# VectorE takes a norm ahead of a sum, the queries' norms move one row block ahead, and the first transfers change their order

## The chip, the cores and the metric

One core of one Trainium2 chip. The metric is device time in microseconds for one execution of the whole program. Engines: PE (TensorE), ACT (ScalarE), DVE (VectorE), POOL (GpSimd), SP (SyncE, which only issues transfers here). They run their own instruction streams and meet at semaphores.

## The reference

One layer of cross-attention and one of experts, all in float32. Cut to the part that the change touches:

```
x: 16 batches x 56 queries x 256;  context: 16 x 1500 x 256, the first 257 rows "image", the other 1243 "text"
q = rms_norm(layernorm(x) @ q_w + q_b) * nq_s          # 16 heads of 128; the mean is over all 2048 columns
for part in (image, text):
    k = rms_norm(part @ k_w + k_b) * nk_s              # 16 heads of 128
    v = part @ v_w + v_b
    out += softmax(q k^T / sqrt(128)) v                # softmax over the rows of that part alone
x = x + out @ o_w + o_b
x = x + experts(layernorm(x))                          # top 4 of 32 experts, and a shared one
```

## The kernel before

The keys and values are never formed. For each head the queries are multiplied by the key weights ("absorbed queries", `u`), so that scores are `context @ u`, and averages are taken over the raw context rows; the value weights follow later. A key row's norm comes from a product of the context row with a Gram matrix of the weights. Float32 operands are split into a high and a low part (fp32r), and each product is three matmuls: high by high, high by low, low by high.

**Stages.** `prologue` (layer norm, Gram matrices), `project` (queries, `u`), the batch loop in `attend`, `outputs`, `experts`. The loop runs from 255 to 1460 us of the span.

**Projection.** `project` goes through 16 heads. For each head, `absorb` computes `u` in four row blocks (two halves of 448 columns each), over four PSUM banks in turn; `order` fixes which unit takes which bank, and `claim` waits until the unit four places before has been copied out. ACT copies half 0 and DVE half 1 (`copy_u`). Near the end three small pieces stand between row blocks: `flip` transposes the sums of squares of the queries, from which DVE and POOL make the norms; `wide` spreads the norms over all partitions, copied out by ACT to `q_rms_wide`; `flat` finds the largest bound on a score, from which DVE judges (`is_safe`) whether the loop must run with maxima. From `q_rms_wide` DVE also makes `beta`, the part of the scores that comes from the key bias. SP stores `beta` in DRAM, loads it back spread over the partitions (`beta_wide`, one transfer for image, one for text), and then copies head 15's first batch of `u` to `u_raw` (L518). POOL scales and splits `u_raw` (`first_rows`) and lets PE begin.

**The loop.** A batch has 13 context tiles of 128 rows: tiles 0 to 2 image (tile 2, `LONE`, has one row), 3 to 12 text. Each tile has two units (448 of the 896 columns of heads by queries), so a batch has 26 steps. At step s the engines do, each in its own order, written out by hand:

- PE: scores of unit s (6 matmuls); at some steps a sum over partitions (`sums`, L1190 and L1191, 2 matmuls); at even steps the Gram product of tile s/2+1 (5 matmuls); the average of unit s-2 (6 matmuls).
- ACT: the exponential of unit s-1, once rounded (`p_high`), once in place; at even steps the high part of a tile (`c_high`).
- DVE: `take` of unit s-1: `p_low` (L1370), the running `p_sum` (L1426 or L1423), and the `seed` that puts beta in a PSUM bank for the scores three units on (L1381); at even steps the `norm` of tile s/2+1 (L1395), which reads the Gram product from PSUM and `c_twice` from SBUF; at steps 1, 2 (text of the batch before) and 7, 8 (image) `split_sum`: the cast `p_sum_high` (L1434), then `p_sum_low` (L1370, two SBUF inputs).
- POOL: at even steps `key_root` (L1558), the power -1/2 of the norm's result, then at most steps one long piece over 896 columns (scaling or splitting `u`, or scaling averages: L1583, L1608, L1621); at odd steps `c_low` (L1564) and `c_twice` (L1577) of a tile.

The Gram product and the sums share one PSUM bank. The sum at step 3 or 9 therefore waits until the norm of step 2 or 8 has read the bank (`norm_summed`), and the sums at 5 and 11 for the norms of 4 and 10. These are `TEXT_SUMS = (3, 5)` and `IMAGE_SUMS = (9, 11)`. DVE takes the norm after `take`, except at step 6, where it comes first.

Of the kernel before, what the change touches and what calls it, by code (L numbers as in the profile page):

```python
# [413 lines left out]
def project(nc, qw_in, kw_in, psum, ident, minus_half, zeros, small, key_scale, bias_high, bias_low, x_high, x_low,  # L414
# [4 lines left out]
    with ctx:  # L419
# [29 lines left out]
        for h in range(H):  # L449
            if h + 2 < H:  # L450
                order += [("q", h + 2, half) for half in range(2)]
            if h == H - 1:
                order += [("wide", half) for half in range(2)]
            for r in range(4):
                if h == H - 2 and r == 2:
                    order += [("flip",)]
                if h == H - 1 and r == 1:
                    order += [("flat",)]
                order += [("u", h, r, half) for half in range(2)]
# [23 lines left out]
        def sync(sp):  # L483
            def load_q(h):
                if h >= LOADS:
                    sp.wait_ge(wq_split, h - LOADS + 1)
                sp.dma_start(wq_stage[:, h % LOADS, :], qw_in[h, :, :]).then_inc(wq_loaded[h % LOADS], 16)

            def load_k(h):
                if h >= LOADS:  # L490
                    sp.wait_ge(wk_split, h - LOADS + 1)
                sp.dma_start(wk_stage[:, h % LOADS, :], kw_in[h, :, :]).then_inc(wk_loaded[h % LOADS], 16)

            def store_u(h):
                sp.dma_start(u_dram[h, :, :, :], u_stage[:, h % U_RING, :, :])\
                    .then_inc(u_stored[h % U_RING], 16)

            for h in range(LOADS):
                load_q(h)
                if h < 2:  # L500
                    load_k(h)
            for h in range(2, LOADS):
                load_k(h)
            for h in range(H):
                if h + LOADS < H:
                    load_q(h + LOADS)
                if 0 < h and h + LOADS - 1 < H:
                    load_k(h + LOADS - 1)
                if h == H - 4:
                    first_tiles[0](sp)  # L510
                if h == H - 1:
                    sp.wait_ge(beta_ready, 1)
                    sp.dma_start(beta_dram, beta[:, :]).then_inc(beta_stored, 16)
                    sp.wait_ge(beta_stored, 16)
                    first_tiles[6](sp)
                sp.wait_ge(u_act, 4 * (h + 1))
                sp.wait_ge(u_dve, 4 * (h + 1))
                sp.dma_start(u_raw[:, :, h * S:(h + 1) * S], u_stage[:, h % U_RING, :, 0:S])\  # L518
                    .then_inc(first_stored[h % U_RING], 16)
                if h < H - U_RING:  # L520
                    store_u(h)

        def sync_stores(sp, s, heads=range(H - U_RING, H)):
# [5 lines left out]
        def tensor(pe):  # L529
# [58 lines left out]

            absorb(H - 2, range(2))
            at = claim(("flip",))  # L590
# [6 lines left out]
            first_tiles[1](pe)  # L597
            absorb(H - 2, range(2, 4))
            for half in range(2):
# [7 lines left out]
                last.then_inc(wide_done, 1)  # L607
            pe.wait_ge(wk_split, H)
            absorb(H - 1, range(1))
            at = claim(("flat",))  # L610
            pe.wait_ge(bound_step, 4)
            nc.tensor.matmul(psum[0:1, at, 0:TOK], bound_max[:, :], ident[0:TOK, 0:TOK], start=True, stop=True)\
                .then_inc(bound_flat, 1)
            absorb(H - 1, range(1, 4))
            pe.wait_ge(beta_ready, 1)
# [4 lines left out]
        def scalar(act):  # L620
# [47 lines left out]
            for h in range(H):  # L668
                if h + 2 < H:
                    take(h + 2)  # L670
                if h + 1 < H:
                    weights_k(h + 1)
                if h + 3 < H:
                    weights_q(h + 3)
                if h == H - 1:
                    for half in range(2):
                        act.wait_ge(wide_done, half + 1)
                        nc.scalar.activation(q_rms_wide[:, cols(half)], psum[:, bank["wide", half], 0:HALF], ACT.Copy)\
                            .then_inc(wide_copied, 1)
                copy_u(h, range(4))  # L680
                if h == H - 3:
                    first_tiles[2](act)

        def vector(dve):
# [39 lines left out]
            for h in range(H):  # L724
# [8 lines left out]
                if h < H - 2:  # L733
# [4 lines left out]
                          psum[0:ROWS_SQ, SUMS:SUMS + 2, 0:HALF]).then_inc(sums_copied, 1)  # L738
            copy_u(H - 2, range(2))
            dve.wait_ge(flipped, 1)  # L740
# [3 lines left out]
                .then_inc(bound_step, 1)  # L744
            copy_u(H - 2, range(2, 4))
            first_tiles[4](dve)
            for step in (1, 2):
# [4 lines left out]
            V.tensor_reduce(bound_max[:, :], bound_sq[:, :], mybir.AxisListType.X, ALU.max).then_inc(bound_step, 1)  # L752
            copy_u(H - 1, range(1))
            dve.wait_ge(bound_flat, 1)
# [8 lines left out]
                            q_rms_wide[0:2 * H, :].rearrange("p (h n) -> p h n", h=2), ALU.mult).then_inc(beta_ready, 1)  # L763
            copy_u(H - 1, range(1, 4))

# [8 lines left out]
def attend(nc, ctx_in, qw_in, kw_in, psum, ident, minus_half, zeros, small, key_scale, bias_high, bias_low, x_high,  # L774
# [4 lines left out]
    with ctx:  # L779
# [29 lines left out]

        def first_betas(sp):  # L810
            for s in range(2):
                sp.dma_start(beta_wide[:, s, :].rearrange("p (h q) -> p h q", h=H),
                             beta_rows[s, :, 0:S].partition_broadcast(P)).then_inc(beta_loaded[s], 16)

# [124 lines left out]
        def _(sp):  # L939
# [159 lines left out]
            with sp.If(unsafe(sp)):  # L1099
                sp.wait_ge(first_split, 9)  # L1100
                for s in range(2):
                    project_stores(sp, s)
                    stored(s)
                with sp.Fori(0, B) as it:
                    maxima(it)
                sp.wait_ge(max_listed, 32 * B + CREDIT["max_listed"])
                for s in range(2):
                    load_u(0, s, u_loaded[s])
                    sp.dma_start(beta_wide[:, s, :].rearrange("p (h q) -> p h q", h=H),
                                 beta_rows[s, :, 0:S].partition_broadcast(P)).then_inc(beta_again, 16)  # L1110
                batches(sp, body_of(False), tail)
            with sp.Else():
# [5 lines left out]
        def _(pe):  # L1118
# [136 lines left out]
            with pe.If(unsafe(pe)):  # L1255
                with pe.Fori(0, B) as it:
                    maxima(it)
                pe.wait_ge(rank_zeroed, 2)
                batches(pe, body_of(False), tail)
            with pe.Else():  # L1260
# [100 lines left out]
        def _(dve):  # L1361
# [99 lines left out]
            def body(it, has_prev, has_next):  # L1461
                for step in range(UNITS):
                    if has_prev and step == 0:
                        take(it - 1, UNITS - 1, True)

                    norms_first = step == 2 * LONE + 2
                    if norms_first:
# [84 lines left out]
        def _(gp):  # L1552
# [114 lines left out]
            for i in range(3):  # L1667
                for k, x in enumerate(first_stored):
                    gp.wait_ge(x, 16 * len([h for h in range(heads[i + 1]) if h % U_RING == k]))
                first_rows(slice(heads[i], heads[i + 1]), 3 * i)  # L1670
            gp.wait_ge(first_split, 9)
            with gp.If(unsafe(gp)):
                with gp.Fori(0, B) as it:
# [3 lines left out]
                gp.wait_ge(first_split, 12)  # L1677
            gp.sem_inc(u_scaled, 2)
            gp.sem_inc(u_high_ready, 2)
            gp.sem_inc(u_split, 2)  # L1680
            batches(gp, body, tail)
# [560 lines left out]
```

## Time and profile before

| | us |
|---|---|
| median of 3 runs | 1937.68 (1935.91 to 1941.32) |
| profiled execution | 1937.42 |
| its span | 1935.3 |
| PE busy | 1774.7 (92%) |
| DVE busy | 1328.5 (69%) |
| POOL busy | 1099.4 (57%) |
| ACT busy | 977.4 (51%) |

The span is the time from the first to the last instruction. Busy time is the sum of an engine's instructions; what counts for the end is which wait ends last at each place, which the timelines below show for one batch of the loop.

### The profile page before, as it was taken

Reading aid. Unit: us, or ns where it says so; the run is one execution under the profiler, and the core shown is the slowest. Engines: PE = TensorE matmul, PEld = TensorE weight load, DVE = VectorE, ACT = ScalarE, POOL = GpSimd, SP = SyncE. Lnnn points to the kernel's source line nnn. Section 1 sums busy time; section 2 is a strip of 40 time slices with the busy share of each in tenths; the row PEclk is TensorE's granted clock in tenths of the full one; section 3 lists DMA queues with packets and bytes.
Section 4 is the critical chain, followed back from the end, with each engine's and each line's share of the span. In section 5 each row is a group of like instructions: output and inputs, shape, how many; then the busy total and the mean of one; then the engine's idle time right before and its main releaser. Section 6 shows DMA issues by size and latency. Waiting matters only on the chain. (4 is left out here: it accounts for less than half of the span.)

```text
span 1935.3 us, 30607 instructions
## 1 busy us (share of the span) xinstructions
PE 1774.7 (92%) x8863; PEld 1563.6 (81%) x8863; DVE 1328.5 (69%) x2522; ACT 977.4 (51%) x1627; POOL 1099.4 (57%) x955
## 2 busy tenths in 40 slices
PE   7899969999999999999999999999992998699998
PEld 7566769889888898898898898898882887588887
DVE  4444457877877777777777768777772565577776
ACT  3444435555655655655555555556552563244443
POOL 1000267778778787788788787787862331133332
PEclk9999989999999999999999999999996999699999
DMA  3355555455555565554464564555435782133332
GB/s 109 126 201 198 193 166 117 109 115 123 117 118 119 125 122 116 121 129 121 101 147 101 113 132 120 114 119 124 101 84 189 250 274 86 61 118 108 121 108 78
DMA packets 417215, 251.17 MB, mean 130 GB/s; under 512 B 350123, under 2 KB 368683, under 8 KB 415372
## 3 DMA queue, kind: packets, MB, share of 16 engines
q1 hardware_dynamic: 417164, 250.54, 50.7%
q8 instruction: 26, 0.43, 0.1%
q14 instruction: 25, 0.20, 0.0%
HBM read 187.70 MB, written 60.10 MB: 128 GB/s over the span
## 5 line engine op out<-in xcount | busy, mean ns | idle before, releaser
L1297 ACT ACTIVATE p_high<-psum,key_rms 128x448 fp32r<-128x448 f32 x384 | 245.1, 638 | 393.1 <-PE psum L1128 393.1
L1370 DVE TENSOR_TENSOR p_low<-psum,p_high 128x448 fp32r<-128x448 f32 x384 | 237.7, 619 | 184.4 <-ACT psum L1299 178.9
L1126 PE MATMUL psum<-u_high,c_high 128*128 128x448 f32 x832 | 307.2, 369 | 26.1 <-DVE psum L1381 13.8
L1128 PE MATMUL psum<-u_high,c_low 128*128 128x448 f32 x832 | 305.6, 367 | 0.0
L1127 PE MATMUL psum<-u_low,c_high 128*128 128x448 f32 x832 | 305.2, 367 | 0.0
L1126 PE MATMUL psum<-p_high,c_high 128*128 128x448 f32 (+1 forms) x768 | 283.5, 369 | 4.1 <-DVE p_low L1370 4.1
L1127 PE MATMUL psum<-p_low,c_high 128*128 128x448 f32 (+1 forms) x768 | 282.2, 367 | 0.0
L1128 PE MATMUL psum<-p_high,c_low 128*128 128x448 f32 (+1 forms) x768 | 281.9, 367 | 0.0
L1564 POOL TENSOR_TENSOR c_low<-stage,c_high 128x512 fp32r<-128x512 f32 x208 | 276.7, 1330 | 0.0
L1381 DVE COPY psum<-beta_wide 128x448 f32<-128x448 f32 x416 | 260.9, 627 | 21.7 <-DMA beta_wide<-absorbed_biases 5.8
L1558 POOL TENSOR_TENSOR key_rms<-key_ms,minus_half 128x1 f32<-128x1 f32 x209 | 117.5, 562 | 244.2 <-DVE key_ms L1395 241.8
L1299 ACT ACTIVATE psum<-psum,key_rms 128x448 f32<-128x448 f32 x384 | 232.6, 606 | 0.0
L1951 POOL TENSOR_TENSOR scaled_gate<-gated,p_wide 128x448 f32<-128x448 f32 x66 | 86.6, 1311 | 193.1 <-ACT gated L2046 157.5
L1426 DVE TENSOR_TENSOR p_sum<-psum,p_sum 128x448 f32<-128x448 f32 (+1 forms) x320 | 196.2, 613 | 0.0
L1126 PEld LDWEIGHTS psum<-u_high,c_high 128*128 128x128 f32 x832 | 156.9, 189 | 46.6 <-DVE psum L1381 16.6
L1127 PEld LDWEIGHTS psum<-u_low,c_high 128*128 128x128 f32 x832 | 157.1, 189 | 13.3
L1128 PEld LDWEIGHTS psum<-u_high,c_low 128*128 128x128 f32 x832 | 157.0, 189 | 13.3
L1577 POOL TENSOR_TENSOR c_twice<-stage,c_low 128x256 f32<-128x256 f32 x208 | 157.9, 759 | 16.4 <-POOL c_low L1564 2.4
L1126 PEld LDWEIGHTS psum<-p_high,c_high 128*128 128x128 f32 (+1 forms) x768 | 143.9, 187 | 17.5 <-DVE p_low L1370 7.5
L1128 PEld LDWEIGHTS psum<-p_high,c_low 128*128 128x128 f32 (+1 forms) x768 | 144.0, 187 | 12.9
L1127 PEld LDWEIGHTS psum<-p_low,c_high 128*128 128x128 f32 (+1 forms) x768 | 144.8, 189 | 10.0
L1395 DVE CUSTOM_DVE_ANT_0 junk<-psum,c_twice 128x257 bf16<-128x257 f32 x208 | 89.0, 428 | 92.9 <-POOL c_twice L1577 74.4
(240 smaller groups left out, 3844.4 us busy)
## 6 DMA issues: line engine op xcount, KB each, us to landing
stage<-in_ctx SPq DMA_DIRECT2D x210, 256.0 KB, 2.8
averages<-o_raw SPq DMA_DIRECT2D x64, 448.0 KB, 5.2
o_stage<-averages SPq DMA_DIRECT2D x32, 896.0 KB, 5.6
u_raw<-absorbed_queries SPq DMA_DIRECT2D x60, 448.0 KB, 5.5
absorbed_queries<-u_stage SPq DMA_DIRECT2D x14, 1792.0 KB, 6.8
beta_wide<-absorbed_biases SPq DMA_DIRECT2D x32, 448.0 KB, 5.1
recip_wide<-reciprocals SPq DMA_DIRECT2D x32, 448.0 KB, 4.1
p_wide<-probs_by_expert SPq DMA_DIRECT2D x32, 448.0 KB, 3.6
```

What stands on the lines that cost most here:

```text
L1126: nc.tensor.matmul(out, high, rhigh, start=start, stop=False, **kw)
L1127: nc.tensor.matmul(out, high, rlow, start=False, stop=False, **kw)
L1128: return nc.tensor.matmul(out, low, rhigh, start=False, stop=stop, **kw)
L1297: nc.scalar.activation(p_high[:, probs_slot(u), :], src, ACT.Exp, scale=key_rms[:, t:t + 1])
L1299: nc.scalar.activation(out, src, ACT.Exp, scale=key_rms[:, t:t + 1]).then_inc(exp_done, 1)
L1370: return nc.vector.tensor_tensor(out, a, b, ALU.subtract)
L1381: nc.vector.tensor_copy(psum[:, bank_of(u), 0:HALF], beta_wide[:, s, cols_of(half)])\
L1395: nc.vector.tensor_tensor_reduce(out=junk[:, :], in0=psum[:, GRAM, 0:DIM + 1], in1=c_twice[:, slot(t, TWICE_RING), :], scale=1.0 / INNER, ...
L1426: added = nc.vector.tensor_tensor(total, part, total, ALU.add)
L1558: nc.gpsimd.tensor_tensor(key_rms[:, t:t + 1], key_ms[:, t:t + 1], minus_half[:, 0:1], ALU.pow)\
L1564: nc.gpsimd.tensor_tensor(c_low[:, k, :], stage[:, st, :], c_high[:, k, :].bitcast(F32), ALU.subtract)\
L1577: nc.gpsimd.tensor_tensor(c_twice[:, slot(t, TWICE_RING), 0:DIM], stage[:, st, nat], c_low[:, k, nat].bitcast(F32), ALU.add).then_inc(stag ...
```

## The change

In `attend`, `norms_first` now holds at steps 2, 4, 8 and 10 beside 6. In `project`, `flip`, `wide` and `flat` each stand one row block earlier on PE, with their partners on ACT and DVE. `first_betas` is called once for each half: the image half where both stood, the text half after the last `u_raw`. POOL's three increments move ahead of its branch; where the branch is taken (it isn't with this data), SP and PE now wait for the last split.

```
             for r in range(4):
-                if h == H - 2 and r == 2:
+                if h == H - 2 and r == 1:
                     order += [("flip",)]
-                if h == H - 1 and r == 1:
+                if h == H - 2 and r == 3:
+                    order += [("wide", half) for half in range(2)]
+                if h == H - 1 and r == 0:
                     order += [("flat",)]
...
                     sp.wait_ge(beta_stored, 16)
-                    first_tiles[6](sp)
+                    first_tiles[6](sp, 0)
                 sp.wait_ge(u_act, 4 * (h + 1))
                 sp.wait_ge(u_dve, 4 * (h + 1))
                 sp.dma_start(u_raw[:, :, h * S:(h + 1) * S], u_stage[:, h % U_RING, :, 0:S])\
...
+            first_tiles[6](sp, 1)
...
-            absorb(H - 2, range(2))
+            absorb(H - 2, range(1))
             at = claim(("flip",))
...
-            absorb(H - 2, range(2, 4))
+            absorb(H - 2, range(1, 3))
             for half in range(2):
                 at = claim(("wide", half))
...
-            pe.wait_ge(wk_split, H)
-            absorb(H - 1, range(1))
+            absorb(H - 2, range(3, 4))
             at = claim(("flat",))
             pe.wait_ge(bound_step, 4)
...
-            absorb(H - 1, range(1, 4))
+            pe.wait_ge(wk_split, H)
+            absorb(H - 1, range(4))
...
-                    norms_first = step == 2 * LONE + 2
+                    norms_first = step % 2 == 0 and (step + 1 in TEXT_SUMS + IMAGE_SUMS or step == 2 * LONE + 2)
                     if norms_first:
                         norm(*ahead(it, step // 2 + 1))
...
             gp.wait_ge(first_split, 9)
+            gp.sem_inc(u_scaled, 2)
+            gp.sem_inc(u_high_ready, 2)
+            gp.sem_inc(u_split, 2)
             with gp.If(unsafe(gp)):
...
-            gp.sem_inc(u_scaled, 2)
-            gp.sem_inc(u_high_ready, 2)
-            gp.sem_inc(u_split, 2)
             batches(gp, body, tail)
```

On DVE, `copy_u` of head 14 is cut at 1 and 3 instead of 2, and that of head 15 is one piece at the end; on ACT the two copies of `wide` stand before block 3 of head 14.

## Rows read from the trace of the kernel before

**Rows 1.** Busy table, loop: us, busy PE, PEld, DVE, ACT, POOL, clock, DMA.
```profile
360.00:1480.00 1120.00, 1053.05 (x5473) 959.80 (x5471) 834.70 (x1697) 623.41 (x1067) 866.48 (x760) 0.99 0.54 117
```
**Rows 2.** Who waited for whom on PE in the loop: us, times, longest.
```profile
PE psum L1190 <- DVE key_ms L1395: 34.0, 31, 1.6
```
**Rows 3.** Timeline, casts beside POOL: start, duration, engine, line; brackets: idle before it.
```profile
486.21 0.74 POOL L1577 TENSOR_TENSOR c_twice<-stage,c_low 128x256 f32<-128x256 f32 x1
486.40 0.81 DVE L1434 CAST p_sum_high<-p_sum 128x448 fp32r<-128x448 f32 x1
...
489.84 0.39 DVE L1434 CAST p_sum_high<-p_sum 128x448 fp32r<-128x448 f32 x1
...
490.00 0.63 POOL L1558 TENSOR_TENSOR key_rms<-key_ms,minus_half 128x1 f32<-128x1 f32 x1 [3.05 <-DVE key_ms L1395]
...
490.26 0.62 DVE L1370 TENSOR_TENSOR p_sum_low<-p_sum,p_sum_high 128x448 fp32r<-128x448 f32 x1
...
490.61 2.27 POOL L1608 TENSOR_TENSOR u_low<-u_raw,u_high 128x896 fp32r<-128x896 f32 x1
```
**Rows 4.** Timeline of steps 2 to 4 around the text sum.
```profile
487.78 0.62 DVE L1370 TENSOR_TENSOR p_low<-psum,p_high 128x448 fp32r<-128x448 f32 x1
...
489.50 0.42 DVE L1395 CUSTOM_DVE_ANT_0 junk<-psum,c_twice 128x257 bf16<-128x257 f32 x1
...
489.98 0.47 PE L1190 MATMUL psum<-p_sum_high,ones_r 128*128 128x448 f32 x1 [0.67 <-DVE key_ms L1395]
...
493.54 0.37 PE L1126 MATMUL psum<-p_high,c_high 128*128 128x448 f32 x1
...
494.98 0.43 DVE L1395 CUSTOM_DVE_ANT_0 junk<-psum,c_twice 128x257 bf16<-128x257 f32 x1 [0.55 <-POOL c_twice L1577]
```
**Rows 5.** Timeline of steps 5 to 8.
```profile
497.05 1.57 DVE L1426 TENSOR_TENSOR p_sum<-lone_probs,p_sum 1x448 f32<-1x448 f32 x1
...
498.09 1.69 POOL L1564 TENSOR_TENSOR c_low<-stage,c_high 128x512 fp32r<-128x512 f32 x1
...
500.62 0.43 DVE L1395 CUSTOM_DVE_ANT_0 junk<-psum,c_twice 128x257 bf16<-128x257 f32 x1 [2.01 <-POOL c_twice L1577]
...
501.65 0.47 PE L1126 MATMUL psum<-u_high,c_high 128*128 128x448 f32 x1 [0.81 <-DVE psum L1381]
```
**Rows 6.** Timeline of steps 8 to 10 around the image sum.
```profile
506.02 0.62 DVE L1370 TENSOR_TENSOR p_low<-psum,p_high 128x448 fp32r<-128x448 f32 x1
...
507.74 0.42 DVE L1395 CUSTOM_DVE_ANT_0 junk<-psum,c_twice 128x257 bf16<-128x257 f32 x1
...
508.22 0.48 PE L1190 MATMUL psum<-p_sum_high,ones_r 128*128 128x448 f32 x1 [1.48 <-DVE key_ms L1395]
...
508.85 2.29 POOL L1583 TENSOR_TENSOR u_raw<-u_raw,rms_batch 128x896 f32<-128x896 f32 x1
...
511.79 0.37 PE L1126 MATMUL psum<-p_high,c_high 128*128 128x448 f32 x1
```
**Rows 7.** Timeline, end of the projection.
```profile
227.79 1.07 DVE L737 COPY square_sums<-psum 33x896 f32<-33x896 f32 x1
```
**Rows 8.** Timeline of the hand-over, and the transfers of L518.
```profile
242.04 2.27 SPq L812 DMA_DIRECT2D beta_wide<-absorbed_biases  x2
242.17 0.62 DVE L716 COPY u_stage<-psum 128x448 f32<-128x448 f32 x1 [0.59 <-PE psum L534]
...
244.41 3.09 SPq L518 DMA_DIRECT2D u_raw<-u_stage  x1
...
251.64 0.42 POOL L1583 TENSOR_TENSOR u_raw<-u_raw,q_rms_wide 128x112 f32<-128x112 f32 x1 [5.11 <-DMA u_raw<-u_stage]
...
252.48 0.42 POOL L1603 TENSOR_TENSOR u_low<-u_raw,u_high 128x112 fp32r<-128x112 f32 x1
...
255.06 0.74 PE L1126 MATMUL psum<-u_high,c_high 128*128 128x448 f32 x1 [12.31 <-POOLq L1680]
...
DMA to landing us min/median/max: 2.2/2.3/7.1
```

More of the change, by code:

```diff
@@ L451, in project @@
                 order += [("q", h + 2, half) for half in range(2)]
-            if h == H - 1:
-                order += [("wide", half) for half in range(2)]
             for r in range(4):
-                if h == H - 2 and r == 2:
+                if h == H - 2 and r == 1:
                     order += [("flip",)]
-                if h == H - 1 and r == 1:
+                if h == H - 2 and r == 3:
+                    order += [("wide", half) for half in range(2)]
+                if h == H - 1 and r == 0:
                     order += [("flat",)]
@@ L674, in scalar @@
                     weights_q(h + 3)
-                if h == H - 1:
+                copy_u(h, range(4) if h != H - 2 else range(3))
+                if h == H - 2:
                     for half in range(2):
@@ L679, in scalar @@
                             .then_inc(wide_copied, 1)
-                copy_u(h, range(4))
+                    copy_u(h, range(3, 4))
                 if h == H - 3:
@@ L738, in vector @@
                           psum[0:ROWS_SQ, SUMS:SUMS + 2, 0:HALF]).then_inc(sums_copied, 1)
-            copy_u(H - 2, range(2))
+            copy_u(H - 2, range(1))
             dve.wait_ge(flipped, 1)
@@ L744, in vector @@
                 .then_inc(bound_step, 1)
-            copy_u(H - 2, range(2, 4))
+            copy_u(H - 2, range(1, 3))
             first_tiles[4](dve)
@@ L752, in vector @@
             V.tensor_reduce(bound_max[:, :], bound_sq[:, :], mybir.AxisListType.X, ALU.max).then_inc(bound_step, 1)
-            copy_u(H - 1, range(1))
+            copy_u(H - 2, range(3, 4))
             dve.wait_ge(bound_flat, 1)
@@ L763, in vector @@
                             q_rms_wide[0:2 * H, :].rearrange("p (h n) -> p h n", h=2), ALU.mult).then_inc(beta_ready, 1)
-            copy_u(H - 1, range(1, 4))
+            copy_u(H - 1, range(4))
         def gpsimd(gp):
@@ L808, in first_loads, with first_betas @@
                 sp.dma_start(stage[:, t, :], ctx_in[t, :, :]).then_inc(ctx_loaded[t], 16)
[L810 to L813, printed above, removed]
+        def first_betas(sp, s):
+            sp.dma_start(beta_wide[:, s, :].rearrange("p (h q) -> p h q", h=H),
+                         beta_rows[s, :, 0:S].partition_broadcast(P)).then_inc(beta_loaded[s], 16)
         def first_gram(pe):
@@ L1110, in _ @@
                                  beta_rows[s, :, 0:S].partition_broadcast(P)).then_inc(beta_again, 16)
+                sp.wait_ge(first_split, 12)
                 batches(sp, body_of(False), tail)
@@ L1258, in _ @@
                 pe.wait_ge(rank_zeroed, 2)
+                pe.wait_ge(first_split, 12)
                 batches(pe, body_of(False), tail)
```

## The prediction

> **What bounds the kernel now.** I read the busy table by stage first, then who waits for whom in the batch loop, then one batch in order of time, then the hand-over into the loop. In the middle of the loop PE is busy 1053.05 of 1120 us, far more than any other engine [rows 1]: it sets the pace, and only what makes PE idle is worth anything. The list of waits names the largest item: 34.0 us in 31 waits, in which the sum's first matmul (L1190) waits for the norm (L1395) [rows 2]. It falls on the first of each pair of sums: 0.67 us at step 3 (text, 15 times) and 1.48 us at step 9 (image, 16 times) [rows 4, 6]. The same places come back in every batch, so one batch stands for all. A wait costs a little more than its idle time: the first matmul after it is recorded 0.10 longer (0.47 for 0.37), and the idle time is counted from the end of the record before, where a matmul otherwise starts every 0.2 us [rows 4]. That is 0.10 + 0.17 each. The ceiling of the loop part is therefore 34 us plus 31 times 0.27, some 42 us.
>
> **Norm first at steps 2, 4, 8 and 10.** No instruction is added; DVE does the same norm at another place, and there it takes the same 0.34 us (489.50 to the next start at 489.84 [rows 3, 4]).
> At step 8 DVE would start it where p_low of unit 7 starts now, at 506.02, and end it at 506.5; PE is ready for the sum at 508.22 - 1.48 = 506.74 [rows 6]. So the 1.48 goes; the norm's two inputs are there by then in the timeline. At step 2 it starts at 487.78 instead of 489.50, with its c_twice done at 486.95 [rows 3], and the 0.67 goes as well [rows 4]. If nothing else moved, this would be the whole 42 us.
> But something else moves. key_root on POOL follows the norm by 0.5 us, and POOL's next long instruction follows key_root by 0.61 (490.00 to 490.61 [rows 3]). At step 2 that is u_low, at step 8 the scaling of u_raw; each takes 2.0 us from where it really starts (u_low is recorded at 490.61 but ends 2.00 after the vector instruction beside it, 490.88) [rows 3, 6]. Today both follow the cast p_sum_high, because the norm stands right before that cast. With the norm first, u_low would run from about 488.8 to 490.9, while DVE still reaches the cast at 489.84. DVE and POOL block each other here. The trace shows it three times: a cast of 0.39 takes 0.81 when it starts at 486.40 inside c_twice (486.21 to 486.95), ending 0.26 after it [rows 3]; the p_sum of the lone row, started at 497.05, ends at 498.62, and c_low, started at 498.09, takes 1.69 and ends 1.16 after that [rows 5]; and key_root, started inside the cast at 490.00, ends at 490.63, in the middle of p_sum_low [rows 3]: POOL had its turn between the two vector instructions.
> This is what the Trainium skill says in "SBUF — State Buffer", section "Who interferes with whom": VectorE in a two-port mode or with two SBUF inputs, and GpSimd, exclude each other for a whole instruction, and the one that issued first goes first. By that rule the trace agrees, and it speaks against this change. Whose turn comes next after a pair, the page doesn't say.
> So at step 2: the cast is held from 489.84 to 490.9 and ends at 491.2. POOL's next instruction, c_low, is by then waiting and takes its turn, 1.16 us, to 492.35. p_sum_low (L1370) then ends at 492.85, not at 490.88, and p_low of unit 2, next on DVE, starts at 492.8 and ends at 493.4. average(2) begins on PE at 493.54 today [rows 4]; without the sum's stall it could begin at 492.6, and now it begins at 493.45. The stall is only handed on.
> Step 8 is the same: the scaling of u_raw runs from 507.05 to 509.2 over the cast at 508.08, c_low takes its turn to 510.6, p_sum_low ends at 511.1, p_low of unit 8 at 511.65; average(8) begins at 511.7, where it begins at 511.79 today [rows 6]. Nothing won.
> What stays: DVE comes to norm 4 (step 4, now first) at 494.5, not at 494.98 [rows 4], for c_twice has come earlier too. key_root, u_low and c_low follow on POOL, so c_twice for step 6 and its norm (500.62, after 2.01 us of waiting for it) come 0.5 to 0.7 earlier, and with them the seed for which PE waits 0.81 at 501.65 [rows 5]. I take 0.6 us in each of 15 batches: 9 us. Step 10 moves likewise and costs nothing: p_low of unit 9 comes after its norm, and average(9) stands over 2 us later in PE's order.
> Bounds: above nothing, if POOL's turn is longer than I think (rival below); at most 42 us plus up to 0.8 us of the wait at 501.65 in 16 batches, 55 us. I stay near the low end because the rows of blocking are the nearest ones.
>
> **Norms of the queries one row block ahead.** The transposition of the square sums (flip), the widened norms (wide) and the flat maximum each move ahead by one row block; PE has the same matmuls before banks_set. The flip may wait for the copy of the square sums, 1.07 us from 227.79 [rows 7]; only its last few tenths are uncovered by the six matmuls of block 0. I cost it at 0, between -1 and +1. What it gives is beta ready about one block earlier: six matmuls at 0.2 us each, 1.2 us, of which I take 1.1. Behind the moved pieces wait ACT's and DVE's copies of block 3 of head 14, and behind those SP's u_raw of head 14 (1 to 2 us later); POOL needs it only after two long pieces of work on heads 0 to 7, so this is hidden.
>
> **First transfers.** Today both beta_wide transfers (issued from 242.04) are ahead of the last u_raw (L518), which SP issues at 244.41 over 3.09 us, and which lands after 7.1 us; other u_raw transfers land in 2.2 to 2.3 [rows 8]. DVE's last copy ends at 242.79, so SP could issue it at 242.85. Then only one beta is ahead of it. Two betas cost 7.1 - 2.3 = 4.8, one 2.4: landing at 242.85 + 2.3 + 2.4 = 247.6 instead of 251.64, 4.1 us. Beta 0 itself, issued 1.1 earlier and alone, must be there and copied twice, which gives about the same time. Bounds: 1 us (only beta's earlier store counts) and 5 us. The text beta comes last, needed first at the seed of unit 6, ten and more us later: free.
> The three sem_inc of POOL move ahead of its branch: u_low ends at 252.90 and PE starts at 255.06 [rows 8]; these 2.16 us go. PE then starts 2 us ahead of POOL's first instruction of the loop, which is the first to be wanted at step 2, so I keep all of it. Sum 6.2, of which I take 5.5: the tile loads on SP move only 1 to 2 us, and the fourth may be late for ACT. The first matmul of the loop takes 0.74 us, twice 0.37, so TensorE stands at the lower of its two levels, 1.2 GHz, after 12.31 us of idle time [rows 8]; some 6 or 7 us of idle time remain, and I leave that price as it is.
> The waits for first_split 12 are in the branch that isn't taken: 0.
>
> **Sum.** The profiled execution took 1937.42 us for a span of 1935.3; the median of the runs is 1937.68, the same within 0.3. 1937.4 - 9 - 5.5 = 1922.9, so 1923 us.
>
> **Rivals.**
> A, the vector pair goes as one: after the blocked cast DVE also gets p_sum_low before POOL's c_low. p_low of unit 2 then ends at 492.4, in time, p_low of unit 8 at 510.65, 1.1 ahead of today. Per batch 1.3 (text, with norm 6) + 1.0 = 2.3, 35 us in all: 1937.4 - 35 - 5.5 = 1897. For it: DVE's two instructions stand 0.42 apart; against it: key_root at 490.00, which got in between [rows 3]. 0.14.
> B, no collision (POOL's instruction comes later than I think, or doesn't block a cast): near the 55 us bound, less 2: 1937.4 - 53 - 5.5 = 1879. Against it the 0.81 us cast [rows 3]. 0.10.
> C, the start alone: norm 6 comes no earlier, because c_low or c_twice is held by DVE instructions that now stand beside it: 1937.4 - 5.5 = 1932. 0.14.
> D, slower: p_sum_low waits for c_low and for c_twice behind it (0.74 [rows 3]). It decides once POOL issues c_twice before the port goes back. Then average(2) begins 0.6 and average(8) 0.7 later than today, and norm 6 0.2 later; PE keeps 0.9 of it per batch: 1937.4 + 14 - 5.5 = 1946. For it: my margin at both averages is only 0.1 us. Against it: c_low needs its own result's semaphore before c_twice. 0.10.
>
> **Chances and range.** Forecast 0.52, A 0.14, B 0.10, C 0.14, D 0.10. The range 1894 to 1934 holds the forecast, A and C, 0.80. The forecast's own range, with the start between 2 and 7 us and the loop between 5 and 14, is 1917 to 1931. Changes under 0.3% (5.8 us, below 1931.9) can't be told from none here. Faster: forecast, A, B and half of C, 0.83; same: the other half of C, 0.07; slower: D, 0.10.
>
> **What would show it.** After the change the row "L1190 waits for key_ms" must be gone or near it. By the forecast PE idles instead before average(2) and average(8), put down to p_low (L1370), some 0.8 and 1.5 us in each batch, p_sum_high (L1434) takes over 1 us at steps 2 and 8 instead of 0.39, and p_sum_low about as long again. The period of a batch, from one image sum to the next, falls by 0.6 us; by A it falls by 2.3, by B by over 3, by C not at all, and by D it rises. The first matmul of the loop (255.06) should come at 249 to 250. The forecast is wrong if p_sum_high keeps its 0.39 at both places, or if a new wait stands before the scores instead of the averages.

## The result, and the profile after

The changed kernel takes 1921.17 us (median of 4 runs, 1920.35 to 1922.58), the kernel before 1939.5 in the same comparison (4 runs, 1935.91 to 1942.01). The ratio is 0.9908, with a 95% interval of 0.9888 to 0.9927. The forecast was 1923 in a range of 1894 to 1934. The profiled span went from 1935.3 to 1919.1 us, so 16.2 us went; the stretches add up as follows, each read from the start of a PE instruction in the two timelines.

| Stretch | before, us | after, us | difference |
|---|---|---|---|
| start to first matmul of the loop | 255.06 | 249.72 | -5.3 |
| first matmul of the loop to last image sum | 1203.92 | 1192.31 | -11.6 |
| last image sum to the end | 476.32 | 477.07 | +0.8 |

The third row lies between 473 and 479 in the profiles of all kernels below, whatever was changed, so it isn't a cost of the change. The loop's part is -0.71 in the period of a batch, 75.04 to 74.33 (from one image sum to the next, the mean of the first 14; the batch shown below has 433.19 to 508.22 [rows 6] and 425.40 to 499.71), times 15, which is -10.6 us, and -1.0 in batch 0 (28.05 to 27.02 from the first matmul to the first image sum).

First the page of after, in the total busy time of each engine:

```profile
span 1919.1 us, 30607 instructions
...
PE 1777.4 (93%) x8863; PEld 1562.5 (81%) x8863; DVE 1373.3 (72%) x2522; ACT 970.6 (51%) x1627; POOL 1101.5 (57%) x955
```

Every count is as before. Yet DVE is busy 44.8 us longer (1328.5 before) on the same 2522 instructions: something holds it inside its instructions. The next row is the middle of the loop, with the columns of [rows 1]:

```profile
360.00:1480.00 1120.00, 1055.76 (x5467) 959.68 (x5466) 876.32 (x1692) 620.61 (x1068) 867.78 (x759) 0.99 0.55 121
```

DVE rose from 834.70 to 876.32, POOL hardly from 866.48 to 867.78. Which instructions took DVE's time, the groups of DVE by line show (count, then busy time and mean ns, then idle time before them):

```profile
L1373 DVE TENSOR_TENSOR p_sum_low<-p_sum,p_sum_high 128x448 fp32r<-128x448 f32 x64 | 69.6, 1088 | 2.2
...
L1437 DVE CAST p_sum_high<-p_sum 128x448 fp32r<-128x448 f32 x64 | 59.4, 928 | 0.0
```

The cast had a mean of 483 ns and p_sum_low of 626. Half of the 64 of each are the second halves of a sum, and these are the ones that grew. The two groups grew by 58.1 us; other DVE instructions became shorter, among them the `p_sum` of the lone row, 1.57 us [rows 5] before and 1.01 now.

Then who waits for whom on PE in the loop (us in total, times, longest us). Beside the row of [rows 2], the kernel before had these two:

```profile
PE psum L1126 <- DVE psum L1381: 13.8, 16, 1.4
PE psum L1126 <- DVE p_low L1370: 4.1, 16, 0.3
```

After the change:

```profile
PE psum L1128 <- DVE p_low L1373: 32.9, 47, 1.3
...
PE psum L1128 <- DVE psum L1384: 4.7, 17, 1.1
```

The row of [rows 2], 34.0 us in 31 waits for the norm, is gone without remainder. In its place stand 32.9 us in 47 waits of the averages for `p_low`, which were 4.1 us before; and the 13.8 us in 16 waits for the seed (the copy of beta into a PSUM bank) came down to 4.7. Together, -34.0 + 28.8 - 9.1 is 14.3 us less of recorded idle time, beside the 11.6 us by which the loop is shorter. One batch shows how. This is the text sum of the batch, on three engines, and answers to [rows 3 to 5]:

```profile
481.59 0.42 DVE L1398 CUSTOM_DVE_ANT_0 junk<-psum,c_twice 128x257 bf16<-128x257 f32 x1
482.10 0.55 POOL L1561 TENSOR_TENSOR key_rms<-key_ms,minus_half 128x1 f32<-128x1 f32 x1 [1.34 <-DVE key_ms L1398]
482.61 2.13 POOL L1611 TENSOR_TENSOR u_low<-u_raw,u_high 128x896 fp32r<-128x896 f32 x1
482.95 0.37 PE L1192 MATMUL psum<-p_sum_high,ones_r 128*128 128x448 f32 x1
483.65 1.34 DVE L1437 CAST p_sum_high<-p_sum 128x448 fp32r<-128x448 f32 x1
484.70 1.44 POOL L1567 TENSOR_TENSOR c_low<-stage,c_high 128x512 fp32r<-128x512 f32 x1
485.03 1.60 DVE L1373 TENSOR_TENSOR p_sum_low<-p_sum,p_sum_high 128x448 fp32r<-128x448 f32 x1
487.21 0.47 PE L1128 MATMUL psum<-p_high,c_high 128*128 128x448 f32 x1 [0.66 <-DVE p_low L1373]
488.26 0.42 DVE L1398 CUSTOM_DVE_ANT_0 junk<-psum,c_twice 128x257 bf16<-128x257 f32 x1
493.77 0.43 DVE L1398 CUSTOM_DVE_ANT_0 junk<-psum,c_twice 128x257 bf16<-128x257 f32 x1 [0.64 <-POOL c_twice L1580]
494.80 0.48 PE L1128 MATMUL psum<-u_high,c_high 128*128 128x448 f32 x1 [0.19 <-DVE psum L1384]
```

Read it from the top. The norm is early and the sum on PE (482.95) no longer waits. But POOL's `u_low` now starts 1.04 us before the cast, and the cast needs 1.34 instead of 0.39: it ends at 484.99, 0.25 after `u_low` (484.74). Now `c_low` goes first and ends at 486.14, 1.15 after the cast; `p_sum_low`, though recorded from 485.03, ends at 486.63. So `p_low` behind it is late and PE waits 0.66 before average(2). What is won comes later: the norm of step 6 waits 0.64 for `c_twice`, where it waited 2.01 [rows 5], and PE waits 0.19 for the seed of the scores, where it waited 0.81.

The image sum, steps 8 and 9, answers to [rows 6]:

```profile
499.71 0.41 PE L1192 MATMUL psum<-p_sum_high,ones_r 128*128 128x448 f32 x1
500.20 2.14 POOL L1586 TENSOR_TENSOR u_raw<-u_raw,rms_batch 128x896 f32<-128x896 f32 x1
501.24 1.34 DVE L1437 CAST p_sum_high<-p_sum 128x448 fp32r<-128x448 f32 x1
502.27 1.46 POOL L1567 TENSOR_TENSOR c_low<-stage,c_high 128x512 fp32r<-128x512 f32 x1
502.62 1.60 DVE L1373 TENSOR_TENSOR p_sum_low<-p_sum,p_sum_high 128x448 fp32r<-128x448 f32 x1
504.81 0.47 PE L1128 MATMUL psum<-p_high,c_high 128*128 128x448 f32 x1 [1.28 <-DVE p_low L1373]
```

The 1.48 before the sum has become 1.28 before average(8), by the same three steps.

The hand-over into the loop answers to [rows 8]:

```profile
243.44 0.61 SPq L518 DMA_DIRECT2D u_raw<-u_stage  x1
244.09 0.63 SPq L813 DMA_DIRECT2D beta_wide<-absorbed_biases  x1
248.16 1.68 DVE L1384 COPY psum<-beta_wide 128x448 f32<-128x448 f32 x3 [4.80 <-DMA beta_wide<-absorbed_biases]
248.19 0.42 POOL L1586 TENSOR_TENSOR u_raw<-u_raw,q_rms_wide 128x112 f32<-128x112 f32 x1 [2.27 <-DMA u_raw<-u_stage]
249.03 0.42 POOL L1606 TENSOR_TENSOR u_low<-u_raw,u_high 128x112 fp32r<-128x112 f32 x1
249.72 0.74 PE L1128 MATMUL psum<-u_high,c_high 128*128 128x448 f32 x1 [6.41 <-POOLq L1677]
```

POOL waits 2.27 us for the last `u_raw` instead of 5.11, and PE begins 0.27 after POOL's `u_low` ends (249.45), where 2.16 us lay between them. PE's idle time fell from 12.31 to 6.41. The price of the low clock behind it stayed nearly the same: the granted clock is 0.50, TensorE's lower level of 1.2 GHz, up to a matmul 5.7 us behind the first in the kernel before (260.78) and 5.0 behind it here (254.69), and the 40th matmul after the first starts 10.17 and 10.26 us after it.

### The profile page after: what moved, and what is told of

Same layout as the page of the kernel before. It is cut to its first block and busy times, and to the rows that moved or that the text cites. A ratio compares the mean times of both kernels' runs of the same rounds, so it can differ in the third digit from the quotient of the medians.

```text
span 1919.1 us, 30607 instructions
## 1 busy us (share of the span) xinstructions
PE 1777.4 (93%) x8863; PEld 1562.5 (81%) x8863; DVE 1373.3 (72%) x2522; ACT 970.6 (51%) x1627; POOL 1101.5 (57%) x955
## 5 line engine op out<-in xcount | busy, mean ns | idle before, releaser
L1128 PE MATMUL psum<-p_high,c_high 128*128 128x448 f32 (+1 forms) x768 | 288.6, 376 | 32.9 <-DVE p_low L1373 32.9
L1580 POOL TENSOR_TENSOR c_twice<-stage,c_low 128x256 f32<-128x256 f32 x208 | 169.5, 815 | 16.3 <-POOL c_low L1567 2.4
L1624 POOL TENSOR_TENSOR o_raw<-o_raw,recip_wide 128x896 f32<-128x896 f32 x64 | 136.0, 2126 | 13.9 <-DMA recip_wide<-reciprocals 13.9
```

What stands on the lines that cost most here:

```text
L1128: nc.tensor.matmul(out, high, rhigh, start=start, stop=False, **kw)
L1580: nc.gpsimd.tensor_tensor(c_twice[:, slot(t, TWICE_RING), 0:DIM], stage[:, st, nat], c_low[:, k, nat].bitcast(F32), ALU.add).then_inc(stag ...
L1624: nc.gpsimd.tensor_tensor(at, at, recip_wide[:, s, cols].unsqueeze(1).to_broadcast([P, 2, HALF]), ALU.mult).then_inc(o_scaled, 1)
```

## The experiments

Unless said otherwise a kernel is timed beside the kernel before, on the same chip, and the ratio is to that one. "Period" is the time from one image sum to the next, as the mean of the first 14.

**The two parts apart.** The first kernel is the kernel before with the order of the norms alone; the second is the changed kernel with that line put back.

```
-                    norms_first = step == 2 * LONE + 2
+                    norms_first = step % 2 == 0 and (step + 1 in TEXT_SUMS + IMAGE_SUMS or step == 2 * LONE + 2)
```

> The kernel before with only the norms ahead of the sums (steps 2, 4, 8, 10). My account: the port between VectorE and GpSimd hands the stall on, the batch period falls by 0.69 us as in the changed kernel, so the loop gives 11 us and the total is 0.9943 of before (1926 to 1930). The first matmul of the loop stays at 255. Rival, that the loop gains only because the start moved: under 3 us, ratio above 0.998.

> The changed kernel with the norms back behind take (only step 6 first): what is left is the projection's order, the transfers and the three increments. My account: first loop matmul at 249.7 instead of 255.1, batch period 75.05 as before, total 5.3 us less, ratio 0.9972. Rival, that the later tile loads give the start back: first matmul at 249.7, but total within 2 us of before.

Norms alone: 1923.37 us, ratio 0.9929 (0.9902 to 0.9956), period 74.32, first matmul of the loop at 255.00 after 12.15 us. Start alone: 1930.7, ratio 0.9964 (0.9954 to 0.9974), period 75.02, first matmul at 251.01 after 6.32. Both totals are lower than expected; in the two profiles the stretch after the last image sum is 473.1 and 473.8 us for 476.3 before, and neither edit touches it. The first matmul of start alone is later than the 249.7 expected because the projection ended later in its profile, at 243.92 for 242.54 (start of its last record). Both parts are worth something by themselves, and the shares 0.71% and 0.36% come to 1.07% against 0.92% for both together, which the intervals allow. Rival C (the start alone matters) falls. Inside batch 0, from the first matmul to the first image sum, the changed kernel takes 27.02 us and norms alone 26.16. That isn't a price of the earlier start as such: start alone takes 27.89, not more than the 28.05 before. The changed kernel has one wait for a seed more there, 0.41 us at 269.31; what brings it is open.

**Does POOL's place matter?** In the changed kernel POOL waits, at step 2 before `split_u` and at step 8 before `scale_u`, until the pair of DVE is through. The norm stays first; only the collision goes.

```
+                    if step == 2:
+                        gp.wait_ge(sum_split, 4 * it + CREDIT["sum_split"])
...
+                    if has_next and step == 8:
+                        gp.wait_ge(sum_split, 4 * it + 2 + CREDIT["sum_split"])
```

> The changed kernel, with GpSimd's long piece at step 2 and at step 8 made to wait for p_sum_low of the second half, so that it can't run over the cast. Port alone (rival): casts back at 0.39 us, average(2) and average(8) in time, 2 us less per batch, some 32 us under the changed kernel. My account has a second bound, GpSimd's own chain norm - key_root - long piece - c_low - c_twice - next norm, 5.3 us long: started later by these waits, it makes norm 4 and norm 10 wait 2 to 2.6 us on VectorE, and the period is 74.5 to 75.0, so 2 to 10 us above the changed kernel though nothing is blocked at the casts.

1934.17 us, ratio 0.9979 (0.9966 to 0.9991), period 75.23. The cast is back at its old length, at this place in the timeline (and 483 ns in the mean):

```profile
484.57 0.39 DVE L1437 CAST p_sum_high<-p_sum 128x448 fp32r<-128x448 f32 x1
...
490.00 0.43 DVE L1398 CUSTOM_DVE_ANT_0 junk<-psum,c_twice 128x257 bf16<-128x257 f32 x1 [2.66 <-POOL c_twice L1580]
490.49 0.47 PE L1192 MATMUL psum<-p_sum_high,ones_r 128*128 128x448 f32 x1 [0.56 <-DVE key_ms L1398]
```

So the long cast is `u_low`'s and the scaling's doing, shown by taking them away. But the loop gained nothing from its shorter DVE instructions: POOL is late, the norm of step 4 waits 2.66 us for `c_twice`, and PE waits again for norms, now before the second sums at 5 and 11. The waits of this kernel, PE's and DVE's own:

```profile
PE psum L1192 <- DVE key_ms L1398: 25.8, 30, 1.3
...
DVE junk L1398 <- POOL c_twice L1580: 124.3, 104, 2.7
```

DVE's waits for `c_twice` are 11.6 us in the changed kernel and 74.4 before. The gain of the edit thus is POOL's earlier chain, not the norm's place; with POOL's chain held back it is gone. The period came out 0.2 above that of before and beyond what was expected (74.5 to 75.0). POOL is held back a little more here than it was before the change: its `u_low` starts 1.90 us after the sum's first matmul (485.77 to 483.87), where it really started 0.90 after it (490.88 to 489.98 [rows 3, 4]), and that matmul had been stalled by 0.67. Whether this is the whole 0.2 isn't shown.

**Which half of the edit?** Norm first at 2, 4 and 6 only.

```
+                    norms_first = step % 2 == 0 and (step + 1 in TEXT_SUMS or step == 2 * LONE + 2)
```

> The changed kernel without the image half of the edit (norm first at 2, 4 and 6, behind take at 8 and 10). My account: at step 8 the stall was only handed from the sum to average(8), so the 1.48 us wait of L1190 comes back, the 1.28 us wait before average(8) goes, and the total is within 2 us of the changed kernel. Rival, that the image norms are worth their wait: 16 times 1.5, 20 us or more above it.

1923.6 us, ratio 0.9923 (0.9899 to 0.9947), period 74.36, against 74.33 with both. PE's waits:

```profile
PE psum L1192 <- DVE key_ms L1398: 23.9, 16, 1.6
...
PE psum L1128 <- DVE p_low L1373: 13.9, 32, 0.7
```

One name of a wait, 23.9 us in 16, is exchanged for the other (19.0 us in 15: 13.9 and 32 times here, 32.9 and 47 in the changed kernel), and no time goes with it; of the 2.4 us in the total 1.8 stand ahead of the loop (first matmul at 251.51 for 249.72). As long as the collision is there, the image half of the edit is worth nothing.

**Take the collision away by moving DVE's pair, not POOL.** Here the second halves' split stands right behind the norm, ahead of `take`. POOL waits for that norm (`key_root` first), so its long instruction can't start before the pair does.

```
                     if norms_first:
                         norm(*ahead(it, step // 2 + 1))
+                    if has_prev and step == TEXT_SUM_SPLIT[1]:
+                        split_sum(it - 1, TEXT, 1)
+                    if step == IMAGE_SUM_SPLIT[1]:
+                        split_sum(it, IMAGE, 1)
                     if step >= 1:
                         take(it, step - 1, has_next)
```

(The old places keep the first halves only.)

> The changed kernel with one more move: at steps 2 and 8 VectorE splits the second half's sum (p_sum_high, p_sum_low) right behind the norm and ahead of take, so that the pair runs in the 1.0 us before GpSimd's long piece starts. My account (the port hands the stall on): both casts back at 0.39 us, p_sum_low at 0.62, average(2) and average(8) without a wait, norm 4 and norm 6 about 1 us earlier; new small waits before average(1) and average(7), whose p_low now comes 0.95 us later. Period 72.7 (72.3 to 73.3), some 26 us under the changed kernel, about 1895. Rival, that p_low is late because of what DVE has in front of it and not because of the port: the wait moves to average(1) and average(7) whole and the period stays at 74.3.

1900.07 us, ratio 0.9804 (0.9787 to 0.982), period 73.01, inside the expected 72.3 to 73.3. In its timeline the pair goes through undisturbed and `u_low` starts behind the cast:

```profile
478.21 0.42 DVE L1398 CUSTOM_DVE_ANT_0 junk<-psum,c_twice 128x257 bf16<-128x257 f32 x1
478.56 0.39 DVE L1437 CAST p_sum_high<-p_sum 128x448 fp32r<-128x448 f32 x1
478.98 0.63 DVE L1373 TENSOR_TENSOR p_sum_low<-p_sum,p_sum_high 128x448 fp32r<-128x448 f32 x1
479.33 2.27 POOL L1615 TENSOR_TENSOR u_low<-u_raw,u_high 128x896 fp32r<-128x896 f32 x1
...
497.05 0.47 PE L1128 MATMUL psum<-p_high,c_high 128*128 128x448 f32 x1 [0.83 <-DVE p_low L1373]
```

The cast's mean is 482 ns and that of `p_sum_low` 626. The move brings 1.32 us per batch (74.33 less 73.01), nearly twice what the edit had brought. The collision cost more than that, since the move has a price of its own: PE's waits for `p_low` fell only to 17.5 us in 33, and 0.83 of them stands at the image's place in each batch, because the pair is now ahead of `take`.

The next kernel is the same with the norm first at steps 2, 6 and 8, no longer at 4 and 10.

```
+                    norms_first = step in (2, 6, 8)
```

> As e5_split_ahead, but at steps 4 and 10 the norm stands behind take again. Asks whether these two are worth anything. My account: VectorE reaches norm 4 about 1 us after its c_twice is there, GpSimd's chain to norm 6 starts 1 us later, and PE's wait for the seed of unit 8 is 0.7 to 1 us longer: period 73.4 to 73.8, 12 to 16 us above e5_split_ahead. Rival, that only steps 2 and 8 count: the same as e5_split_ahead within 2 us.

1913.29 us, ratio 0.9864 (0.9847 to 0.988), period 73.74. The order at 4 and 10 is worth 0.74 us per batch, and PE shows where:

```profile
PE psum L1128 <- DVE p_low L1373: 17.5, 33, 0.8
...
PE psum L1128 <- DVE psum L1384: 12.1, 16, 1.1
```

The waits for `p_low` are the same; the seed of unit 6 is late, 12.1 us in 16, as it was before the change (0.72 at 492.21 in the batch shown, where the norm of step 6 waits 2.00 for `c_twice` at 491.18). So the path of the gain is norm of step 4, POOL's chain, `c_twice`, norm of step 6, seed. Steps 4 and 10 weren't taken apart; the wait that comes back is the one behind step 4.

**POOL's turn between the pair.** The second halves' low part is left out, in the changed kernel: `p_sum_low` and its matmul (0.4 us of matmuls per batch). The output lacks the low part of those sums. If `c_low` took its turn only because the pair came in two instructions, the long cast stays and the rest goes.

```
                 nc.vector.tensor_copy(p_sum_high[:, half, :], ...).then_inc(sum_high_ready, 1)
...
+                if half == 1:
+                    dve.sem_inc(sum_split, 1)
+                    return
```

> The changed kernel without p_sum_low of the second halves and without the matmul that reads it (the sums of the second halves lose their low part). Takes away the instruction that waits for c_low's turn; the blocked cast stays at 1.34 us. My account: average(2) and average(8) start without a wait, 0.93 and 1.55 us, 0.4 us of matmuls less, the seed's wait gone: period 71.2 (71.0 to 71.8). If the cast's own blocking were what makes p_low late, the waits would shrink only by p_sum_low's plain 0.55 us: period 73.0 or more.

1878.67 us, ratio 0.9695 (0.9679 to 0.9712), period 71.47. The cast, here at step 2, is as long as in the changed kernel, and PE waits for `p_low` no more than before the change:

```profile
476.21 1.33 DVE L1441 CAST p_sum_high<-p_sum 128x448 fp32r<-128x448 f32 x1
...
PE psum L1128 <- DVE p_low L1377: 4.4, 17, 0.3
```

(The first line is the timeline's, the second the list of waits.) Without its second member the pair costs PE nothing: the 0.95 us of the cast alone are hidden. Of the 2.86 us by which the period fell, 0.4 are the matmuls left out, 1.9 the waits of 0.66 and 1.28, and 0.2 the seed's wait of 0.19, which is gone too. The other 0.3 is about what three waits cost beyond their idle time if it is 0.10 each, the length by which the first matmul after a wait is recorded longer; that is an estimate.

**The start, in its two pieces.** The kernel before with POOL's increments ahead of its branch (and the two waits in the branches not taken), and the changed kernel with the increments behind it.

```
             gp.wait_ge(first_split, 9)
+            gp.sem_inc(u_scaled, 2)
+            gp.sem_inc(u_high_ready, 2)
+            gp.sem_inc(u_split, 2)
             with gp.If(unsafe(gp)):
...
-            gp.sem_inc(u_scaled, 2)
-            gp.sem_inc(u_high_ready, 2)
-            gp.sem_inc(u_split, 2)
             batches(gp, body, tail)
```

> The kernel before with only GpSimd's three increments ahead of its branch. My account: the first matmul of the loop at 252.9 instead of 255.06 (2.1 us), period unchanged at 75.05, total 2 us less; the other 3.2 us of the start come from the transfers. Rival, that PE then waits for something else (the seeds): first matmul after 254.

> The changed kernel with the three increments back behind GpSimd's branch: the transfers and the projection's order alone. PE's idle time before the first matmul of the loop was 12.3 us before and is 6.4 in the changed kernel; the increments alone left 10.4. My account, that the two add up: 8.3 us here. Rival, that the earlier transfer is hidden by the branch or by the seeds: over 10 us.

Increments alone: 1937.61 us, ratio 0.9994 (0.9984 to 1.0004), no difference that can be told, and the first matmul at 255.44 where 252.9 was expected. All but them: 1921.48 (2 runs), ratio 0.9914 (0.9896 to 0.9933), against 0.9908 with them. So in the total time the increments show no gain; what they do is seen only in the hand-over. The last matmul of the projection and the first of the loop, in the kernel with increments alone:

```profile
244.28 0.78 PE L617 MATMUL psum<-q_high 128*128 128x448 f32 x3
255.44 0.74 PE L1127 MATMUL psum<-u_high,c_high 128*128 128x448 f32 x1 [10.39 <-POOLq L1676]
```

and the first matmul in the other:

```profile
253.03 0.74 PE L1128 MATMUL psum<-u_high,c_high 128*128 128x448 f32 x1 [7.58 <-POOLq L1683]
```

By PE's idle time the increments take off 1.9 us (12.31 to 10.39), the transfers with the projection's order 4.7 (12.31 to 7.58), both together 5.9 (to 6.41): they don't add up, since with the transfers in place the increments bring 1.2 (8.3 us of idle time was expected without them, not 7.58). The gap between the end of POOL's last `u_low` and PE's first matmul shows why: it is 2.16 us before, 0.26 with the increments alone and 0.27 in the changed kernel, but 1.54 in the kernel with all but them (251.49 to 253.03), so less was left to win; what shortened it there is open. The start of the first matmul is a worse measure than the idle time, because the projection's last record starts at 241.97, 242.54, 244.28 and 244.67 in these four profiles (before, changed, increments alone, all but them). The edit doesn't account for that: with the same code of the projection it lies between 241.97 and 244.28 in the three profiles with the old order, and between 241.99 and 244.67 in the nine with the new one, while PE's idle time is 6.24 to 6.46 us in all eight that have both pieces of the start.

**A version that beats both.** If the pair costs only where it delays `p_low` before an average, it should stand where no average is near: each second half one norm later, at steps 4 and 10, behind that norm. The lines of the kernel of 1900.07 us that put the split behind the norm are in this one too; the constants move it:

```
-        TEXT_SUM_SPLIT, TEXT_SUMS, TEXT_RECIP = (1, 2), (3, 5), 10
-        IMAGE_SUM_SPLIT, IMAGE_SUMS, IMAGE_RECIP = (7, 8), (9, 11), 16
+        TEXT_SUM_SPLIT, TEXT_SUMS, TEXT_RECIP = (1, 4), (3, 5), 10
+        IMAGE_SUM_SPLIT, IMAGE_SUMS, IMAGE_RECIP = (7, 10), (9, 11), 16
```

> As e5_split_ahead, but the second half's split stands right behind the norms of steps 4 and 10 instead of 2 and 8. There VectorE waits 0.7 us for c_twice anyway, and the 1.0 us before GpSimd's long piece is free as well. My account: no blocked cast (0.39) and p_sum_low 0.62 there, the waits before average(1) (0.16) and average(7) (0.83) gone with their restarts, the wait before average(6) stays at 0.29: period 71.6 to 71.9, 18 us under e5_split_ahead, about 1881. Rival, that average(3) and average(9) now wait in their place: period stays at 73.0.

1885.48 us (1881.46 to 1889.53), ratio 0.9734 (0.9715 to 0.9752), period 72.03, just above the expected 71.6 to 71.9. The timeline of the text pair at its new place, and the middle of the loop in the columns of [rows 1] (one stretch, 360 to 1400):

```profile
480.43 0.43 DVE L1398 CUSTOM_DVE_ANT_0 junk<-psum,c_twice 128x257 bf16<-128x257 f32 x1 [1.37 <-POOL c_twice L1584]
480.78 0.39 DVE L1437 CAST p_sum_high<-p_sum 128x448 fp32r<-128x448 f32 x1
481.20 0.62 DVE L1373 TENSOR_TENSOR p_sum_low<-p_sum,p_sum_high 128x448 fp32r<-128x448 f32 x1
481.54 2.28 POOL L1615 TENSOR_TENSOR u_low<-u_raw,u_high 128x896 fp32r<-128x896 f32 x1
...
360.00:1400.00 1040.00, 1036.11 (x5394) 942.42 (x5393) 810.53 (x1673) 606.05 (x1050) 846.41 (x749) 1.00 0.57 122
```

PE is busy 1036.11 of 1040 us there, 99.6%; in the kernel before it was 1053.05 of 1120, 94.0%. Little is left for the order of work to win in the loop. PE's waits for `p_low` are 4.4 us in 17, as before the change, and those for the seed 1.1 in one, though DVE itself waits 76.8 us for `c_twice` in this kernel. The kernel is 35.7 us faster than the changed one (1885.48 to 1921.17; by the two ratios to the kernel before, 34), by moving one pair of DVE instructions in each of the two sums.

## Why the prediction was right

**Sum.** Forecast 1922.9 from 1937.4 - 9 - 5.5; the span fell by 16.2, where 14.5 was the sum. Both steps are right in sign and mechanism, and both sizes are near, the second partly by luck (below).

**The wait removed** was the right one: the row of [rows 2] is gone. That it would not pay out was the step that mattered, and it held in its details:

| Step of the forecast | forecast, us | measured, us |
|---|---|---|
| cast at steps 2 and 8 | over 1 | 1.34 and 1.34 |
| `c_low` has its turn before `p_sum_low`, ends after the cast | 1.16 | 1.15 |
| `p_sum_low` ends after `c_low` | 0.50 | 0.49 |
| wait before average(2) | 0.8 | 0.66 |
| wait before average(8) | 1.5 | 1.28 |
| period | -0.6 | -0.71 |
| first matmul of the loop | 249 to 250 | 249.72 |

Taking POOL's instruction from beside the cast brought the cast back to 0.39, and moving the pair gave 1.32 us per batch, so that this is shown and not only argued. The Trainium skill says in "SBUF — State Buffer", section "Who interferes with whom", that a VectorE instruction in a two-port mode or with two SBUF inputs and a GpSimd instruction exclude each other for a whole instruction: the cast of 1.34 us that ends 0.25 after `u_low` agrees. Rival A, the vector pair going as one, would have been the reading if two DVE instructions 0.04 us apart went through together; the rows show that they don't.

Both waits came out 0.1 to 0.2 below the forecast, and so did the price that it put on a wait beyond its idle time, 0.27: against the changed kernel the last version of the experiments has 2.1 us less of recorded idle time per batch in three waits fewer (0.66, 0.19 and 1.28), and its period is 2.30 shorter, which leaves some 0.06 for each (0.1 by the kernel without the low part). The ceiling of 42 us, which counts 31 of them, was thus too high by some 5 to 6 us.

**What stays of it** was forecast as POOL's chain coming earlier and with it norm 6 and the seed: the seed's wait fell from 0.81 to 0.19, 0.62 us, where 0.6 was taken. The kernels with POOL held back (gain gone, +0.9 per batch) and without the order at 4 and 10 (0.74 lost per batch) show this path.

**The term that was mis-sized** is the loop's: 9 us was forecast and 11.6 measured. 1.6 us of it is the period (0.71 for 0.6, 15 times). The other 1.0 is batch 0, which the forecast counted with nothing; the norms alone bring 1.9 us there (28.05 to 26.16 between the first matmul and the first image sum), with the earlier start beside them 1.0 is left, and why is open.

**The start** was taken at 5.5 and came to 5.3 on the first matmul. Its pieces come out as forecast when each is read against the last record of the projection in its profile (241.97 before, 242.54 after):

| Piece | forecast, us | measured, us |
|---|---|---|
| beta's multiplication on DVE, from 2.92 to 4.14 ahead of that record | 1.1 | 1.2 |
| POOL takes up the last `u_raw`, from 9.67 to 5.65 behind it | 4.1 | 4.0 |
| gap between POOL's `u_low` and PE's first matmul, 2.16 to 0.27 | 2.16 | 1.9 |

The first row works through the second and isn't added to it. The last two are the 5.9 by which PE's idle time fell; the record itself starts 0.6 later, which makes 5.3. The forecast came from 6.2 to 5.5 by another reason, late tile loads, which no run shows; that 5.5 and 5.3 agree so well is luck by these 0.6 and 0.7 us. "I keep all of it" for the increments was the weak step: beside the transfers they bring 1.2 to 1.3, not 2.16.

**Rivals.** B fell with the cast of 1.34, C with the norms' 0.9929 and a period shorter by 0.72, D with the seed's wait being shorter rather than longer; POOL's `c_twice` did not come before `p_sum_low` again.

## What to carry to other kernels

When a wait on an ordering is taken out, ask what the moved instruction also releases on the other engines, and lay that engine's next long instruction against what now stands beside it: here the norm released POOL, and POOL's 2 us fell on a DVE pair, which returned 29 of the 34 us. When two DVE instructions belong together and a long POOL instruction waits behind a DVE result, put the pair right behind that result and ahead of POOL's start, at a step where PE's next need of DVE is far off; that was worth some 35 us here, about twice the whole change. Take the names in a list of waits as places and not as causes: the name changed from the norm to `p_low` with no time moved at the image sum, and the 76.8 us of DVE's waits for `c_twice` in the kernel of 1885 us cost PE next to nothing.

## What the runs showed of the hardware

A POOL instruction that waits gets its turn between two DVE instructions that are recorded 0.04 us apart: `c_low`, which started on record at 484.70 inside the cast, ended at 486.14, before `p_sum_low` at 486.63. A blocked pair thus costs 2 us (1.34 + 1.60 for 0.39 + 0.62), not the 1 us of the first block. In this program the second of the pair waits on a semaphore of the first; whether two DVE instructions without such a wait between them would go through together, no run tested.

Moving the three increments ahead of POOL's branch, which isn't taken, took 1.2 to 1.9 us off PE's idle time (7.58 to 6.41 and 12.31 to 10.39), and no time off the whole that could be told. And the last record of the projection, in the same code, started anywhere from 241.99 to 244.67 us in nine profiles, so that a gain of 1 us in it can't be read from one profile.
